# A first cross-attention written anew: transposed reciprocals behind the V products, two folds and the weight rounding on GpSimd

## The reference, cut to what matters

```python
x = x + tanh(g_xattn[0]) * L0_xattn(layernorm(x), ctx)   # 16 heads of 16, 77 keys
x = x + tanh(g_ffn[0])   * L0_ffn(layernorm(x))          # ternary weights
x = x + tanh(g_xattn[1]) * L1_xattn(x, ctx)              # 8 heads of 64
x = x + tanh(g_ffn[1])   * L1_ffn(x)

# L0_xattn(q, k, v):
qh, kh, vh = heads(q @ wq.T + bq), heads(k @ wk.T + bk), heads(v @ wv.T + bv)
attn = softmax(einsum('bhqd,bhkd->bhqk', qh * SCALE, kh))
out  = einsum('bhqk,bhkd->bhqd', attn, vh)
return merge(out) @ wo.T + bo
```

## Time and profile before

| what | value |
|---|---|
| median of 3 runs | 2057.97 us (2052.27 to 2058.33) |
| profiled execution, its own time | 2059.8 us |
| its span | 2057.9 us |
| mean granted TensorE clock | 0.963 |
| busy PE / PEld / DVE / ACT / POOL | 1865.6 / 1522.4 / 1206.2 / 1123.3 / 710.3 us |

### The profile page before, as it was taken

How to read it: one execution, slowest core, us unless ns; L and a number is a source line. 1 busy time by engine, 2 the same in 40 slices (tenths; PEclk the granted TensorE clock), 3 DMA queues, 4 the chain that set the end, 5 groups by cost and what they waited for, 6 DMA issues and landing times. The chain is left out here.

```text
span 2057.9 us, 61748 instructions
## 1 busy us (share of the span) xinstructions
PE 1865.6 (91%) x27201; PEld 1522.4 (74%) x27201; DVE 1206.2 (59%) x1656; ACT 1123.3 (55%) x1942; POOL 710.3 (35%) x821
## 2 busy tenths in 40 slices
PE   4888959999999999998699986899999999999986
PEld 3666748887888888886578765778888878787865
DVE  6888623324324233242555435888888888787882
ACT  4777623434434344342455533677777777766661
POOL 3666710010000100010333321556656565564441
PEclk9999979999999999999799997999999999999997
DMA  5221010000000000000201004312332232223110
GB/s 168 83 95 44 22 36 1 21 1 21 21 1 20 11 10 20 0 20 26 91 27 34 18 26 129 94 56 65 101 95 60 65 110 85 65 76 99 55 44 24
DMA packets 135939, 104.92 MB, mean 51 GB/s; under 512 B 9379, under 2 KB 132104, under 8 KB 135688
## 3 DMA queue, kind: packets, MB, share of 16 engines
q1 hardware_dynamic: 135688, 101.19, 16.3%
HBM read 76.00 MB, written 25.17 MB: 49 GB/s over the span
## 5 line engine op out<-in xcount | busy, mean ns | idle before, releaser
L1557 ACT ACTIVATE E_prob<-E_ps_s,E_negmax 128x1024 f32<-128x1024 f32 x256 | 284.7, 1114 | 145.2 <-DVE E_negmax L1871 144.8
L1871 DVE TENSOR_REDUCE E_negmax<-E_ps_s 128x1 f32<-128x1024 f32 x256 | 301.5, 1219 | 90.0 <-PE E_ps_s L1376 89.8
L1878 DVE STREAM_TRANSPOSE E_prob<-E_prob 128x1024 f32<-128x1024 f32 x256 | 303.9, 1225 | 23.8 <-ACT E_prob L1557 11.4
L1395 PEld LDWEIGHTS E_ps_o<-E_prob,E_vrep 32*64 32x64 f32 x15872 | 232.4, 131 | 71.1 <-ACT E_part L1583 55.2
L1395 PE MATMUL E_ps_o<-E_prob,E_vrep 32*64 32x128 f32 x15872 | 265.0, 274 | 18.1 <-issue 9.0
L979 ACT ACTIVATE F_raw<-F_ps,ffn_scales 128x512 f32<-128x512 f32 x128 | 88.2, 689 | 288.2 <-PE F_ps L889 288.2
L889 PE MATMUL F_ps<-F_ha,ffn_w_rounded 128*128 128x512 f32 x1024 | 240.5, 396 | 0.0
L889 PE MATMUL F_ps<-F_hb,ffn_w_rounded 128*128 128x512 f32 x1024 | 240.2, 396 | 0.0
L889 PEld LDWEIGHTS F_ps<-F_hb,ffn_w_rounded 128*128 128x128 f32 x1024 | 192.6, 188 | 46.3
L889 PEld LDWEIGHTS F_ps<-F_ha,ffn_w_rounded 128*128 128x128 f32 x1024 | 191.5, 188 | 47.7 <-issue 1.6
L1773 POOL TENSOR_TENSOR E_part<-E_part 128x512 f32<-128x512 f32 x93 | 119.3, 1283 | 255.2 <-ACT E_part L1583 255.2
(11 more groups left out here) (273 smaller groups left out, 3943.2 us busy)
## 6 DMA issues: line engine op xcount, KB each, us to landing
E_vrep<-E_v_all SPq DMA_DIRECT2D x128, 256.0 KB, 3.0
A_w_stage<-in_L_ffn_h_wT SPq DMA_DIRECT2D x16, 512.0 KB, 4.4
E_v_all<-E_vst SPq DMA_DIRECT2D x32, 256.0 KB, 2.2
F_x<-x SPq DMA_DIRECT2D x9, 512.0 KB, 3.7
A_x<-in_x SPq DMA_DIRECT2D x16, 256.0 KB, 5.2
x<-A_x SPq DMA_DIRECT2D x16, 256.0 KB, 2.2
x<-F_x SPq DMA_DIRECT2D x8, 512.0 KB, 2.9
C_x<-x SPq DMA_DIRECT2D x16, 256.0 KB, 5.9
```

The costliest lines, as they stand in the source:

```text
L1395: mm = pe.matmul(low[64 * j:64 * j + 64, g, :], vrep[rows, slot, KB // 4 * (quarter % 2) + k, dh * j:dh * (j + 1)], prob[rows, u % 2, :, j ...
L1557: act.activation(prob[:, s // UT % 2, s % UT, j, :], ps_s[:, j, :], ACT.Exp, bias=negmax[:, at:at + 1], scale=1.0, accum_out=den[:, 2 * c ...
L1871: dve.tensor_reduce(negmax[:, at:at + 1], ps_s[:, j, :], AX.X, ALU.max, negate=True).then_inc(d_max, 1)
L1878: dve.transpose(at, at).then_inc(d_t, 1)
```

## The change

Stage A gets a function of its own, `first_attention`. The other stages are as before; `cross_attention` loses the parts that only stage A used. What is different in stage A:

- `normalize` is gone. The transposes of P wait for `exp`, and P keeps three buffers instead of four.
- `recip_sum` goes behind `shift`. GpSimd folds twice (624 elements a row, then 320), and VectorE sums the 320.
- GpSimd spreads the reciprocals over the 16 columns of each head (`widen`), TensorE transposes them for a pair (`reciprocals`), ScalarE evacuates them (`r_evacuate`), and VectorE multiplies the products with V by them (`weigh`), which replaces ScalarE's evacuation of o.
- The weight chunks are rounded on GpSimd (`round_chunk`), in the steps of a list, five in eight steps; VectorE's `mantissas` go by the same list. The verdict is read in step 29 (`JUDGED = 31`).
- The root of batch 0 runs on VectorE; `k_evacuate(0)` and the gates' tanh come ahead of the steps; `v_proj(0)` goes behind the first scores.
- SyncE's order of loads is new: two pairs of x, the context and wk first; three chunks before x of pair 4; context of batch b+2 at the second pair of a batch.

The core of the diff:

```diff
-CHECK_FROM = -4
-JUDGED = 28
+CHUNK_STEPS = (-5, -4, -3, -2, -1, 1, 3, 4, 5, 7, 9, 11, 12, 13, 15, 17, 19, 20, 21, 23, 25, 27)
+JUDGED = 31
...
+def first_attention(nc, ident, gates, gates_src, x_src, x_dst, ctxT, wqT, wkT, wvT, woT, bias, H, ffn, tag):
...
+        def v_step(b):
+            return 2 * PB * b - 3 if b else -2
...
+            load_x(0)
+            load_x(1)
+            load_ctx(0)
+            load_w(0, wk, wkT)
+            for dst, src in ((qbias[:, :], bq), (kbias[:, :], bk)):
+                sp.dma_start(dst, src).then_inc(s_small, 16)
+            load_x(2)
+            load_x(3)
+            load_w(2, wq, wqT)
+            for i, g in enumerate(gates_src):
+                sp.dma_start(gates[:, i, :], ...).then_inc(s_gates_in, 16)
+            load_w(1, wv, wvT)
+            for dst, src in ((vbias[:, :], ...), (obias[:, :], ...)):
+                sp.dma_start(dst, src).then_inc(s_wide, 16)
+            for i in range(STAGE):
+                load_chunk(i)
+            for n in range(PB, 2 * PB):
+                load_x(n)
+            load_w(3, wo, woT)
+            load_ctx(1)
+            load_chunk(STAGE)
+            for n in range(2 * PB, XR):
+                load_x(n)
+            at = STAGE + 1
+            for n in range(NP):
+                if n % PB == 1 and n // PB + 2 < B:
+                    b = n // PB + 2
+                    sp.wait_ge(e_v, b - 1)
+                    load_ctx(b)
+                while at < CHUNKS and CHUNK_STEPS[at - STAGE] <= 2 * n + 2:
+                    load_chunk(at)
+                    at += 1
...
+            def reciprocals(n):
+                pe.wait_ge(p_wide, 2 * n + 2)
+                if n:
+                    pe.wait_ge(d_fin, n)
+                else:
+                    pe.wait_ge(x_taken, 4)
+                for c in range(C):
+                    for t in range(2):
+                        each = r_wide[:, (2 * n + t) % RS, HC * c:HC * (c + 1), :].rearrange("p h w -> p (h w)")
+                        at = c * PAIR + t * TOK
+                        mm = pe.transpose(ps_m[:, at:at + TOK], each, ident[:, :])
+                mm.then_inc(e_r, 1)
...
+            def q_proj(n):
+                pe.wait_ge(x_taken, n + 1)
+                if n >= 3:
+                    pe.wait_ge(r_taken, n - 2)
...
+            def p_transpose(T, g):
+                pe.wait_ge(a_exp, T + 1)
...
+            for T in STEPS:                                   # TensorE
+                n, odd = divmod(T, 2)
+                if 0 <= T + 2 < TILES:
+                    scores(T + 2)
+                if T == v_step(0):
+                    v_proj(0)
+                if 0 <= T < TILES:
+                    for g in range(G // 2):
+                        p_transpose(T, g)
+                if odd and 0 <= n - 1 < NP:
+                    reciprocals(n - 1)
+                if not odd and 0 <= n + 2 < NP:
+                    x_transpose(n + 2)
+                if 0 <= T < TILES:
+                    for g in range(G // 2, G):
+                        p_transpose(T, g)
+                if odd and 0 <= n + 2 < NP:
+                    q_proj(n + 2)
+                if 0 <= n - 1 < NP:
+                    pv(n - 1, odd)
+                if not odd and 0 <= n - 2 < NP:
+                    out_proj(n - 2)
...
+            def r_evacuate(n):
+                act.wait_ge(e_r, n + 1)
+                if n:
+                    act.wait_ge(o_out, n)
+                act.activation(rt[:, :, :], ps_m[:, :].rearrange("p (c w) -> p c w", c=C), ACT.Copy).then_inc(r_taken, 1)
...
+            def fold(T):
+                pool.wait_ge(a_exp, T + 1)
+                if T:
+                    pool.wait_ge(p_quarter, T)
+                own.step(pool.tensor_tensor(half_sum[:, :, 0:S2 // 2], prob[:, T % PR, :, 0:S2 // 2],
+                                            prob[:, T % PR, :, S2 // 2:S2], ALU.add))
+                if T >= 2:
+                    pool.wait_ge(d_r, T - 1)
+                pool.tensor_tensor(quarter[:, T % 2, :, :], half_sum[:, :, 0:HALF // 2],
+                                   half_sum[:, :, HALF // 2:HALF], ALU.add).then_inc(p_quarter, 1)
+
+            def widen(T):
+                pool.wait_ge(d_r, T + 1)
+                if T >= RS:
+                    pool.wait_ge(e_r, (T - RS) // 2 + 1)
+                by_place = rsum[:, T % RS, :].rearrange("p (g c j) -> p c g j", c=C, j=HR)
+                for c in range(C):
+                    ins = pool.tensor_copy(r_wide[:, T % RS, HC * c:HC * (c + 1), :].rearrange("p (g j) w -> p g j w", j=HR),
+                                           spread(by_place[:, c, :, :].unsqueeze(3), 3, dh))
+                ins.then_inc(p_wide, 1)
...
+            def round_chunk(i):
+                pool.wait_ge(s_chunk[i % STAGE], 16 * (i // STAGE + 1))
+                pool.tensor_copy(ffn.w[:, i * WCH:(i + 1) * WCH], w_stage[:, i % STAGE, :]).then_inc(p_rounded, 1)
...
+            for T in STEPS:                                   # GpSimd
+                if (T + 8) % 8 < 3 and 1 <= (T + 8) // 8 < B:
+                    root((T + 8) // 8, (T + 8) % 8)
+                if 0 <= T + 2 < TILES:
+                    fold(T + 2)
+                if 0 <= T < TILES:
+                    widen(T)
+                if odd and 0 <= n < NP:
+                    add_bias(n)
+                if T in CHUNK_AT:
+                    round_chunk(CHUNK_AT[T])
...
+            def weigh(n):
+                dve.wait_ge(e_pv, n + 1)
+                dve.wait_ge(r_taken, n + 1)
+                if n >= 2:
+                    dve.wait_ge(e_y, n - 1)
+                dve.tensor_tensor(ot[:, n % 2, :, :], ps_o[:, :, :], rt[:, :, :], ALU.mult).then_inc(o_out, 1)
...
+            for T in STEPS:                                   # VectorE
+                if not odd and 0 <= n - 2 < NP:
+                    weigh(n - 2)
+                if 0 <= T + 2 < TILES:
+                    row_max(T + 2)
+                if T + 2 == JUDGED:
+                    judge()
+                if 0 <= T + 2 < TILES:
+                    shift(T + 2)
+                if 0 <= T + 1 < TILES:
+                    recip_sum(T + 1)
+                b, p = divmod(T + 12, 8)
+                if p < PB and b < B:
+                    ln_stats(PB * b + p)
+                if T == 0:
+                    dve.wait_ge(s_gates, 1)
+                for b in range(B):
+                    if T == v_step(b):
+                        v_evacuate(b)
+                if not odd and 0 <= n - 2 < NP:
+                    residual(n - 2)
+                if T in CHUNK_AT:
+                    mantissas(CHUNK_AT[T])
```

More of the change, by code:

```diff
@@ L253, in _ @@
                 load_x(n)
-            if ffn:
-                for i in range(4 - CHECK_FROM):
-                    load_chunk(i)
             for n in range(NP):
[L258 to L262, removed]
                 if n % PB == 0 and n and n // PB + 1 < B:
@@ L338, in scores @@
                     pe.wait_ge(d_sub, T)
-                if ffn and T == JUDGED:
-                    pe.wait_ge(d_worst, 1)
-                    pe.transpose(ps_s[0:1, 0, 512 - P:512], w_worst[:, :], ident[:, :]).then_inc(e_worst, 1)
                 for c in range(C):
@@ L531, in _ @@
                     layer_norm(n + 3)
[L532 to L535, removed]
                 if T == -2 and SPLIT:
@@ L683, in residual @@
                                          op0=ALU.mult, op1=ALU.add).then_inc(d_fin, 1)
[L685 to L697, removed]
-                own.step(dve.tensor_scalar(w_bits[:, :], w_bits[:, :], MANTISSA, None, ALU.bitwise_and))
-                dve.tensor_reduce(w_worst[:, :], w_bits[:, :], AX.X, ALU.max).then_inc(d_worst, 1)
             dve.memset(prob[:, :, :, S:S2], 0.0).then_inc(s_pad, 1)
@@ L710, in _ @@
                     row_max(T + 2)
-                if ffn and T + 2 == JUDGED:
-                    dve.wait_ge(e_worst, 1)
-                    dve.tensor_reduce(ffn.inexact[0:1, 0:1], ps_s[0:1, 0, 512 - P:512], AX.X, ALU.max).then_inc(d_inexact, 1)
                 if 0 <= T + 1 < TILES:
@@ L751, in _ @@
                     residual(n - 2)
-                if ffn and 0 <= T - CHECK_FROM < CHUNKS:
-                    mantissas(T - CHECK_FROM)
-                if ffn and T == CHECK_FROM + CHUNKS:
-                    mantissa_found()
-            if ffn:
-                dve.wait_ge(d_inexact, 1)
 class FfnWeights:
@@ L2039, in gated_layers @@
                 fw.w = w
-                cross_attention(nc, ident, gates[:, 0, 0:1], t["x"], x1, t["ctxT"],
+                first_attention(nc, ident, gates, (t["g_xattn"], t["g_ffn"]), t["x"], x1, t["ctxT"],
                                 *(t[f"L0_xattn_{n}T"] for n in ("wq", "wk", "wv", "wo")),
-                                tuple(t[f"L0_xattn_{n}"] for n in ("bq", "bk", "bv", "bo")), None, 16, "A",
-                                (gates, t["g_xattn"], t["g_ffn"]), fw)
```

(1 more changed line is left out.)

441 lines of the change are left out of this document (419 added, 22 removed).

## The result

The changed kernel takes 2043.5 us (median of 7 runs, 2040.5 to 2047.6), the kernel before 2055.0 (7 runs, 2049.4 to 2058.3). The ratio is 0.9946, 95% interval 0.9929 to 0.9963: 11.5 us faster by the medians, 8 to 15 by the interval. Forecast were 2040 and 18 us.

A forecast was written before the change was run, and what follows sets the result against it. A ring through three engines held stage A's earlier steps and TensorE paced the late ones; gains of 14 (29 steps), 2.2 (start) and 1.5 (end) made 18 us, so 2040 against a median of 2058, range 2024 to 2052.

The forecast's parts named there:

- What bounds it: Stage A's 29 steps: TensorE paces late steps, a ring through three engines earlier ones; after the change TensorE, 6.06 a step.
- TensorE's floor: Rival, stage A: VectorE's unevenness is absorbed, all 29 steps take 6.06, 182 instead of 208.3 us; 2028 in all; chance 0.20.
- Normalising goes: GpSimd in stage A: 71.9 us leave it; no time gained by itself beyond the waits it removes.
- the shift's move: VectorE, stage A: shift ahead of recip_sum takes the sum's 0.80 and the reciprocal off the path scores, row max, shift.
- the rival of mutual locks: GpSimd and VectorE in stage A: all 17 ORs take 2.20 instead of 1.69, +9 us; 2049 in all; chance 0.20.
- 3 us a batch, 9 in three: VectorE in each batch's last four steps: 29 us of work against TensorE's 25, TensorE at most a step ahead.
- the chunks' move: Rounding 22 chunks: ScalarE loses 23.1 us, nothing gained there; GpSimd takes 1.6 a chunk, 27 us for 17.
- 194 forecast: Stage A's 29 steps: 182 for TensorE, 9 for VectorE's unevenness, 3 for the lower clock; gain 14 from 208.3.
- Start: Stage A up to scores 2: earlier root, K evacuation and later V products bring them at 35.4 instead of 37.6; gain 2.2.
- End: Stage A behind scores 31: ring gone, four transposes and the product added; 22.5 instead of 24.0 us, gain 1.5.
- the ring: Stage A's earlier steps: scores, row max, shift, exp, fold, sum, normalize, transposes wait in a circle through three engines.

The follow-up runs named there:

- both: Changed kernel with the root of batches 1 to 3 in two steps instead of three and the verdict one step earlier: 2031.2 us, ratio 0.9885 to the kernel before.
- The two swaps of order: Kernel before with shift ahead of sum and reciprocal: 2069.2 us, ratio 1.0075; changed kernel with sum and reciprocal ahead of shift: 2048.4 us, ratio 0.9976.

## Why the prediction was right, and which of its terms were off

**What bounds it.** Right. TensorE's list sets 6.09 us a step once nothing holds it up, against 6.06 forecast, and K and V products 1.0 each. The kernel "both" comes within 4 us of the floor of 182.6. The rival "TensorE's floor" so had the bound right too; what kept the changed kernel off it were the waits below.

**Normalising goes.** Right: the waits of GpSimd for the reciprocal and of the transposes for GpSimd are gone. The two swaps of order show that the order within VectorE was not what held the kernel before back: it is a loss of 12.9 us there and a gain of 4.7 in the changed kernel. That `normalize` alone makes this difference is argued from its waits, not run. The forecast named the shift's move as a part with a value of its own. It has one only together with the other.

**Prices.** The second fold took 0.957 us (0.94 forecast), the sum 0.477 (0.48), `weigh` 0.688 (0.69), a group of four reciprocal transposes some 0.6, the widening 0.52 for its two copies, which overlap (0.65). The chunk copy took 1.056 us, where I had taken 1.6 between the bounds of 0.96 and 2.40: nearly the lower one. The Trainium skill (GPSIMD Engine Reference, Engine selection), by which one-input work runs there at about line rate, had given an estimated 0.9; the trace agrees more with it than with my middle value. The OR took 1.41 instead of 1.69, probably since the operation of 2.25 us that it collided with in the earlier trace rows is gone; the rival of mutual locks, with 2.20, was wrong in sign. Over the 29 steps VectorE was busy 159.9 us, with the forecast at 168, and GpSimd 139.2, with 152.

**The term that failed in kind: "3 us a batch, 9 in three".** This was VectorE's unevenness. The changed kernel loses 0.7 a batch there, 2.1, and without any OR 3.0 us less in the 29 steps. I had added up the engine's work over four steps, and that sum says little: the run with a chunk in every step lost 6.8 us in two steps, since there two steps in a row had too much ahead of `weigh` and the row max.

**What it left out.** Two waits in the queues, 7.4 us for the root and 3.6 for the verdict, each proved by the edit that removes it. The forecast priced the chunks' move by their own duration and the verdict's not at all; it didn't ask what stands behind a chunk on GpSimd, or ahead of `mantissa_found` on VectorE. They filled the 7 us of overcharge and more: 194 forecast, 198.5 measured. So the sum was near for partly wrong reasons: by luck, one term too dear stood against two that were missing. The whole of stage A is the same: 18 us forecast and 14.0 measured, with the start 2.8 better, the steps 4.5 and the end 2.3 worse.

**Start.** 5.0 instead of 2.2. The root of batch 0 ended at 14.2 instead of 15.6, scores 0 came at 21.8 instead of 23.4, scores 2 at 32.6 instead of 35.4. How much of the 5.0 belongs to the change is open by some 2.6 us, for with the same start code "both" had scores 2 at 35.19, 2.4 earlier than the kernel before and close to the forecast. The mechanism was as forecast, and the second x transpose waited for `v_evacuate` as forecast:

```profile
14.00 0.24 DVE L612 TENSOR_SCALAR A_rs<-A_rs 128x8 f32<-128x8 f32 x1
...
21.79 0.81 PE L348 MATMUL A_ps_s<-A_kt,A_q 32*128 32x154 f32 x16 [0.93 <-ACT A_q L452]
...
26.77 0.63 PE L304 MATMUL A_ps_m<-ident,A_xn 128*128 128x128 f32 x4 [3.16 <-DVE A_vcol L655]
...
32.60 0.81 PE L348 MATMUL A_ps_s<-A_kt,A_q 32*128 32x154 f32 x16 [0.93 <-ACT A_q L452]
```

The early K evacuation is worth 1.3 us at the first transposes, the place of the V products nothing. The rest would be the loads' new order and the root on VectorE; I didn't part these two.

**End.** -0.8 instead of +1.5: this term failed in sign. In the last steps, in which one engine waits for the other, the changed kernel took 24.7 us at a granted clock of 0.93, and the kernel before 24.0 at 0.93. So at the same mean clock the end became longer. Presumably the transposes and the product that were added to it cost more than the ring's going gave back; no run parts them. Even at 1.00 it took 23.3 us, not 22.5. Right behind the 3.5 us in which TensorE waited for the verdict, eight transposes took 1.74 us that take 1.10 elsewhere, but where the clock falls in this stretch differs between runs, and the forecast had no term for it.

**From stage A to the median.** Of 14.0 us in the stage 11.5 are seen in the medians. The profiled execution of before lies 4.8 us over the median of its seven runs, where the three runs that I had gave 1.8. That is within the scatter of single runs. The forecast of 2040 also stood on a median of 2058 from three runs, which seven runs put at 2055: from there a gain of 18 would have been 2037.

## What to carry to other kernels

An order that hurts while an operation stands in a ring of engines waiting for one another can pay once the operation is out: try the two together too, and not the order alone. When work moves into an engine's queue, look at each step for what stands behind it there and who waits for that, for an engine with 70 us of idle time can still hold up all others by 3 us at one place, and an engine's busy sum over several steps shows neither. Short work of the next stage did best here in steps that left the one ahead of the last statistics free, and on the engine whose next operation nobody was waiting for.

## What the runs showed of the hardware

**Small VectorE operations are held up by GpSimd too.** In the changed kernel the first of the small operations on the variances starts beside a fold:

```profile
33.74 1.51 POOL L530 TENSOR_TENSOR A_half_sum<-A_prob 128x624 f32<-128x624 f32 x1 [1.08 <-ACT A_prob L477]
33.81 1.48 DVE L601 TENSOR_SCALAR A_rs<-A_mv 128x8 f32<-128x8 f32 x1
```

In the kernel "both" (its VectorE lines stand one further down), where the fold begins after them, the same operation takes 0.17 us, and the OR that follows meets the fold instead:

```profile
35.82 0.17 DVE L602 TENSOR_SCALAR A_rs<-A_mv 128x8 f32<-128x8 f32 x1
...
36.34 1.51 POOL L530 TENSOR_TENSOR A_half_sum<-A_prob 128x624 f32<-128x624 f32 x1 [1.66 <-ACT A_prob L477]
36.38 2.55 DVE L674 TENSOR_TENSOR A_w_bits<-A_w_bits,A_w_stage 128x1024 int32<-128x1024 int32 x1
```

A one-input operation on 8 elements a partition thus takes some 1.3 us longer. The Trainium skill (SBUF — State Buffer, Who interferes with whom) names such operations among those that can take the shared ports; the trace agrees.

**The clock in a serial end varies between runs of kernels that end alike.** From scores 31 to the last residual the granted clock of the changed kernel and its variants was 1.00 (23.3 and 23.9 us), 0.93 to 0.94 (24.6 to 24.9), 0.90 (25.6) or 0.83 to 0.84 (27.1 and 27.3). The last output projection, eight matmuls, took 1.99 us, or 3.64 in the kernel "both", where TensorE hadn't waited for the verdict. That is up to 4 us which no edit here was made to change.

**A chunk's cast costs the same on both engines**: 1.056 us on GpSimd and 1.050 on ScalarE for 128x1024.
